# Storing only the two 16x16 diagonal blocks of each Gram product, in place of 32x32 blocks

## The chip, the cores and the metric

The kernel runs on one core of one Trainium2 chip. The metric is the device time of one execution, in microseconds (us). A core has five engines with queues of their own: PE (TensorE, matrix products; PEld is its loading of weights), DVE (VectorE), ACT (ScalarE), POOL (GpSimd) and SP (SyncE, which here only issues transfers). Each works through its instructions in order, and they wait for each other through semaphores. SBUF is the on-chip memory of 128 partitions, PSUM the banks into which PE writes, and DMA engines move data between them and the main memory (HBM).

## The reference

`x` has the shape (16, 64, 256, 256): batch, channels, rows, columns. Two layers are applied:

```
x = x + spectral_conv(group_norm(x))     # FFT, 32x17 modes mixed per head of 16 channels, inverse FFT, bias
x = x + whiten(group_norm(x))            # the last axis (256 columns) in 16 groups of 16
```

The whitening takes, over all batches, channels and rows, the covariance of each group of 16 columns:

```
fg = (x_flat - mean).reshape(16 groups, 16, n)
cov = einsum('gmn,gkn->gmk', fg, fg) / (n - 1)
cov = ((1 - 0.001) * cov + 0.001 * eye) / (n - 1)
out = solve(cholesky(cov), fg)
```

So only 16 blocks of 16x16 are needed of the 256x256 matrix of products of columns (the Gram matrix).

## The kernel before, in words

The kernel has three long stages, with short ones between.

**The first pass** runs over 64 units (a unit is one batch and one head of 16 channels, in 8 pairs). SP loads `x_in` in four parts of 1 MB per unit into one buffer; a part is loaded again as soon as the unit before has used it (`loads`, line 283). For each pair PE makes the Gram products of 32 columns with themselves (`products`, line 421: bank 0 for pairs 0 to 3, bank 1 for pairs 4 to 7), then the transform over rows (line 432) of a sum and a difference of halves that DVE (`halves_sum`, line 854) and POOL (line 768) have made, then the transposes (line 440) and the transform over columns (line 454). Both DVE and POOL may write the halves of pair q only when PE has done line 432 of pair q-2. ACT copies the transformed rows out of PSUM (line 645), DVE the transposes (`xt_copy`, line 860) and, once per unit, the spectrum (`spectrum_kept`, line 866), which PE must have before line 454 of the next unit's first pair. PE runs one pair behind with line 440 and two behind with line 454.

Each unit's Gram products stand in `gram`, 128 partitions x (8 pairs x 2 halves x 32 columns). Partition p holds row p % 32 of a block, and its 32 columns are two runs of 16, of which only one belongs to the row's own group of 16. ACT copies them out of PSUM in two pieces (after pairs 3 and 7) and stores all 512 columns with one transfer at the end of the unit (line 679). Before it overwrites `gram` at pair 3 of the next unit it waits for that transfer and for DVE (`diag_done`). DVE multiplies `gram` by a table of unit matrices (`diagonal`, line 872, at pair 0 of the next unit) and sums the rows (`diagonal_sum`, line 877, at pair 4): the sums of squares for the group norm. At pair 7 ACT issues eight small transfers of the spectrum of the unit before (`spectra_out`, line 653).

DVE's `ch(...)` is an instruction with a wait for its own end behind it, so that the next one may read what it wrote.

**Between**, the modes are mixed, and the second group norm's factors are found.

**The second pass** reads the stored half-transformed rows back (`crs`, SP line 352, two transfers of 512 KB per unit, two buffers), multiplies them on PE (line 525), and reads `gram` back (SP line 356, 256 KB per unit). POOL scales the Gram products by the unit's factors (line 797) and adds them up in `gacc` (line 801). SP's order per unit is: two parts of `crs`, then `gram_in`, for which it waits until POOL is through with the buffer.

**The third pass** loads `x` again, whitens it and stores the output. The change leaves it as it is.

The order on every engine is written out by hand, in the loops shown here.

## Time and profile before

| | |
|---|---|
| median of 3 runs | 3546.78 us (3540.39 to 3562.65) |
| the profiled execution's own time | 3551.07 us |
| its span | 3549.2 us |
| first pass | from the start to about 1141 us |
| second pass | about 1444 to 1706 us |
| third pass | about 1750 us to the end |
| PE, DVE, ACT, POOL busy | 2906.7, 2531.4, 1146.2, 1121.2 us |
| moved by DMA | 1001.81 MB, of it 64 stores and 64 loads of 256 KB for `gram` |

The busy times are sums over the whole span; which engine another waits for is to be read in each pass by itself. A busy time includes the time in which an instruction has been started and is held up.

### The profile page before, as it was taken

What the parts mean: (1) busy time and instruction counts of PE and PEld (TensorE: products, weight loads), DVE (VectorE), ACT (ScalarE), POOL (GpSimd) and SP (SyncE); (2) the same over time, 40 slices, a digit from 0 to 9 for tenths busy, and PEclk for the clock granted to TensorE, in tenths of its full rate; (3) what the DMA queues carried; (4) which work ended last, traced back from release to release, by engine and by line L of the source; (5) the groups of instructions that cost most, each with busy time, mean ns of one, the idle gap of its engine ahead of it and who ended that gap; (6) DMA issues with size and microseconds to landing.
All of it is one profiled execution on the core that took longest, in us unless ns stands there. A gap on an engine that the chain in (4) does not pass through costs nothing.

```text
span 3549.2 us, 230090 instructions
## 1 busy us (share of the span) xinstructions
PE 2906.7 (82%) x98565; PEld 2043.7 (58%) x98565; DVE 2531.4 (71%) x4358; ACT 1146.2 (32%) x2860; POOL 1121.2 (32%) x1434
## 2 busy tenths in 40 slices
PE   4888888888887342466499999999999999999998
PEld 2555555555554331122277777777777777777776
DVE  2777777777777335655477777777777777777777
ACT  0222222222221221000144444444444444444444
POOL 2666666666666112455111111111111111111111
PEclk7999999999999555699799999999999999999999
DMA  9999999999998661699388888888888888888887
GB/s 217 323 330 331 328 331 328 328 331 330 327 328 261 87 91 19 197 339 338 121 302 301 300 303 301 301 301 303 300 301 301 303 301 301 301 303 301 301 302 278
DMA packets 630257, 1001.81 MB, mean 282 GB/s; under 512 B 103712, under 2 KB 464176, under 8 KB 630192
## 3 DMA queue, kind: packets, MB, share of 16 engines
q1 hardware_dynamic: 528816, 912.44, 78.3%
q10 hardware_dynamic: 101376, 88.39, 8.7%
q8 instruction: 55, 0.90, 0.1%
q14 instruction: 10, 0.08, 0.0%
HBM read 639.40 MB, written 361.28 MB: 282 GB/s over the span
## 4 chain that ended last, share of the span: by engine, by line
PE 49%; issue 15%; ACT 14%; ACTq 10%; DMA 6%; DVE 5%; SPq 2%; DVEq 0%; POOL 0%; POOLq 0%
PE bank L593 15%; ACT reg L645 13%; PE bank L584 11%; ACTq L653 6%; PE bank L421 5%; DMA reg<-xh_d 5%; PE bank L432 5%; PE bank L440 3%; PE bank L454 3%; PE bank L564 2%; PE bank L501 2%; PE bank L525 2%; SPq L293 1%; ACT xh L645 1%; PE bank L463 1%
## 5 line engine op out<-in xcount | busy, mean ns | idle before, releaser
L645 ACT ACTIVATE reg<-bank 128x512 f32<-128x512 f32 (+3 forms) x1696 | 844.9, 529 | 1100.9 <-PE bank L593 941.3
L1064 DVE STREAM_TRANSPOSE reg<-bank 128x256 f32<-128x256 f32 x2048 | 737.9, 417 | 336.7 <-PE bank L610 336.7
L768 POOL TENSOR_TENSOR reg<-reg 128x512 f32<-128x512 f32 x512 | 690.0, 1348 | 442.2 <-PE bank L432 386.9
L1068 DVE SCALAR_TENSOR_TENSOR reg<-reg,m,mwhit 128x1024 f32<-128x1024 f32 x512 | 657.6, 1284 | 72.1 <-DVE reg L1064 38.1
L593 PE MATMUL bank<-tab,reg 64*128 64x256 f32 x4096 | 691.9, 404 | 0.0
L822 POOL TENSOR_TENSOR reg<-reg,tab 128x64 f32<-128x64 f32 x512 | 164.2, 321 | 1550.2 <-ACT reg L645 828.5
L854 DVE TENSOR_TENSOR reg<-reg 128x512 f32<-128x512 f32 x512 | 529.1, 1034 | 55.2 <-DMA reg<-in_x_dram 29.7
L610 PE MATMUL bank<-reg 32*32 32x128 f32 x32768 | 547.4, 279 | 1.7 <-DVE reg L1064 1.7
L610 PEld LDWEIGHTS bank<-reg 32*32 32x32 f32 x32768 | 370.8, 103 | 210.3 <-issue 171.5
L584 PE MATMUL bank<-tab,reg 64*128 64x64 f32 x8704 | 443.5, 235 | 46.2 <-ACT reg L645 46.1
L593 PEld LDWEIGHTS bank<-tab,reg 64*128 64x128 f32 x4096 | 458.2, 187 | 27.8 <-issue 0.7
L645 ACT ACTIVATE xh<-bank 128x256 f32<-128x256 f32 x512 | 190.2, 383 | 833.0 <-PE bank L432 730.6
L584 PEld LDWEIGHTS bank<-tab,reg 64*128 64x128 f32 x8704 | 373.0, 147 | 146.5 <-ACT reg L645 112.1
L421 PE MATMUL bank<-reg 128*32 128x32 f32 x32768 | 390.8, 199 | 48.8 <-DMA reg<-in_x_dram 24.6
L860 DVE COPY xht<-bank 128x256 f32<-128x256 f32 x512 | 217.0, 424 | 254.3 <-PE bank L440 248.4
L421 PEld LDWEIGHTS bank<-reg 128*32 128x32 f32 x32768 | 344.2, 110 | 65.4 <-issue 56.3
L432 PE MATMUL bank<-reg,tab 128*32 128x256 f32 x4096 | 332.9, 392 | 6.9 <-issue 5.3
L440 PE MATMUL bank<-tab,xh 128*128 128x128 f32 x1024 | 226.5, 303 | 69.1 <-ACT xh L645 69.1
L440 PEld LDWEIGHTS bank<-tab,xh 128*128 128x128 f32 x1024 | 103.4, 141 | 291.7 <-issue 166.9
L525 PE MATMUL bank<-reg 128*64 128x290 f32 x1024 | 165.9, 454 | 95.1 <-DMA reg<-xh_d 81.2
L572 PE MATMUL bank<-tab,reg 34*128 34x256 f32 x1024 | 228.9, 377 | 0.4 <-ACT reg L645 0.4
L454 PE MATMUL bank<-tab,xht 128*32 128x34 f32 x8192 | 174.1, 202 | 60.3 <-DVE reg L866 54.5
(121 smaller groups left out, 1760.0 us busy)
## 6 DMA issues: line engine op xcount, KB each, us to landing
reg<-in_x_dram SPq DMA_DIRECT2D x256, 1024.0 KB, 8.4
reg<-in_x_dram SPq DMA_DIRECT2D x512, 512.0 KB, 3.9
out_dram<-reg SPq DMA_DIRECT2D x512, 512.0 KB, 2.9
xh_d<-xh ACTq DMA_DIRECT2D x128, 512.0 KB, 7.0
reg<-xh_d SPq DMA_DIRECT2D x128, 512.0 KB, 5.9
gram_d<-gram ACTq DMA_DIRECT2D x64, 256.0 KB
reg<-gram_d SPq DMA_DIRECT2D x64, 256.0 KB, 5.1
spec_d<-psu ACTq DMA_DIRECT2D x512, 8.5 KB
```

What stands on the lines that cost most here:

```text
L421: ins = mm(bank[q // 4][BL * j:BL * j + BL, at:at + BL], blk, blk, start=q % 4 == 0 and half == 0 and c == 0 and t == 0, stop=c == 1 and t ...
L432: ins = mm(bank[2 + q % 2][row:row + KX, 0:W], hc[:, par], halves[:, q % 2, par, c], **one)
L440: ins = mm(bank[4 + q % 2][:, P * half:P * half + P], xh[:, q, P * half:P * half + P], T("eye"), start=half == 0, stop=True, is_transpose= ...
L454: ins = mm(bank[6][BL * j:BL * j + BL, KW * q:KW * q + KW], xht[:, q % 4, half, BL * j:BL * j + BL], wj[:, half], start=q == 0 and half == ...
L584: ins = mm(bank[2 + c][:, at:at + KH], x_re[k, q, r, P * half:P * half + P], T("eye")[k, k], start=half == 0 and r == 0, stop=False, is_tr ...
L593: ins = mm(bank[2 + c][:, H * half:H * half + H], z_sb[k, q // 2, q % 2, P * half:P * half + P], T("hb")[k], start=False, stop=True, skip_ ...
L610: ins = mm(bank[4 + j][BL * i:BL * i + BL, P * half:P * half + P], wp[r, e, half], xt_sb[r, e, half, i // 2].rearrange("p (n h) -> p n h", ...
L645: copy = lambda o, i, **k: nc.scalar.activation(o, i, ACT.Copy, **k)
L768: nc.gpsimd.tensor_tensor(out=halves[:, q % 2, 1], in0=x_in[:, 2 * q:2 * q + 2, 0], in1=x_in[:, 2 * q:2 * q + 2, 1], op=ALU.subtract).then ...
L854: v.tensor_tensor(out=halves[:, q % 2, 0], in0=x_in[:, 2 * q:2 * q + 2, 0], in1=x_in[:, 2 * q:2 * q + 2, 1], op=ALU.add).then_inc(S["sum_m ...
L1064: ins = v.transpose(o_sb[:, q].rearrange("p n (f w) -> p f n w", f=2)[:, :, :, BL * j:BL * j + BL], bank[4 + j][:, 0:W].rearrange("p (f n ...
L1068: v.scalar_tensor_tensor(out=o_sb[:, q], in0=o_sb[:, q], scalar=m1[:, ds(t * 4 + q, 1)], in1=mwhit[:, :].unsqueeze(1).to_broadcast([P, 4, W]),
```

## The change

What is stored shrinks from 2x32 to 2x16 columns per pair: `gram_d`, `gram_in`, `gram_w`, `gacc` and `cov` are half as wide. DVE picks the run of 16 columns that belongs to a row's own group: one instruction multiplies the first run by a column `lo` (1 in partitions of the first 16 of 32, else 0), a second adds the other run times `hi`. Both write `blocks`, one half of `gmask`; the unit matrix is then multiplied into the other half, `diag`. The store moves from the end of the unit to pair 3 of the next one, behind DVE's `blocks_made`; DVE waits for the store of the unit before ahead of overwriting `blocks`. The instruction that adds the last cross terms to `cov` becomes two.

```
-COLS = dict(hc=KH, wj=2 * KW, hb=H, e0=W, e1=W, rot=P, fold=KW + 1, eye=P, eye32=2 * BL, dc=1, hk=1, hh=1,
+COLS = dict(hc=KH, wj=2 * KW, hb=H, e0=W, e1=W, rot=P, fold=KW + 1, eye=P, eye32=2 * BL, eye16=2 * M, lo=1, hi=1, dc=1, hk=1, hh=1,
...
+    put("eye16", np.tile(np.eye(M), (P // M, 2)))
+    low_row = (np.arange(P) % BL < M).astype(float)[:, None]
+    put("lo", low_row)
+    put("hi", 1.0 - low_row)
...
-    gram_d = nc.dram_tensor("gram_d", (NU, P, PAIRS * 2 * BL), f32, kind="Internal").ap()
+    gram_d = nc.dram_tensor("gram_d", (NU, P, PAIRS * 2 * M), f32, kind="Internal").ap()
...
-        gram_in, a = cut(reg3, a, 2, PAIRS * 2 * BL)
-        gram_w, a = cut(reg3, a, PAIRS * 2 * BL)
+        gram_in, a = cut(reg3, a, 2, PAIRS * 2 * M)
+        gram_w, a = cut(reg3, a, PAIRS * 2 * M)
...
-        gacc, a = cut(reg3, a, PAIRS * 2 * BL)
+        gacc, a = cut(reg3, a, PAIRS * 2 * M)
+        diag, blocks = (gmask_f[:, i * 256:i * 256 + 256].rearrange("p (n f b) -> p n f b", f=2, b=M) for i in range(2))
...
+            def gram_out(u):
+
+                act.wait_ge(*nth("blocks_made", u + 1))
+                act.dma_start(gram_d[ds(u, 1)].rearrange("u p a -> (u p) a"),
+                              gmask_f[:, 256:512]).then_inc(S["gram_out"], 16)
...
                     if q % 4 == 3:
                         j = q // 4
-                        if j == 0:
-                            act.wait_ge(*nth("gram_out", u * 16))
-                            act.wait_ge(*nth("diag_done", u))
+                        if j == 0 and not first:
+                            gram_out(u - 1)
...
-                act.wait_ge(*nth("gram_copied", u * 2 + 2))
-                act.dma_start(gram_d[ds(u, 1)].rearrange("u p a -> (u p) a"),
-                              flat(gram[:, :, :])).then_inc(S["gram_out"], 16)
...
+            gram_out(NU - 1)
             spectra_out(NU - 1)
...
                 dve.wait_ge(*nth("gram_copied", u * 2 + 2))
-                ch(v.tensor_tensor(out=gmask[:, :, :], in0=gram[:, :, :],
-                                   in1=T("eye32").unsqueeze(1).to_broadcast([P, PAIRS, 2 * BL]), op=ALU.mult))
-                dve.sem_inc(S["diag_done"], 1)
+                dve.wait_ge(*nth("gram_out", u * 16))
+                g = gram[:, :, :].rearrange("p n (f s b) -> p n f s b", f=2, s=2)
+                ch(v.tensor_scalar(blocks, g[:, :, :, 0], T("lo"), None, ALU.mult))
+                ch(v.scalar_tensor_tensor(out=blocks, in0=g[:, :, :, 1], scalar=T("hi"), in1=blocks,
+                                          op0=ALU.mult, op1=ALU.add))
+                dve.sem_inc(S["blocks_made"], 1)
...
             def diagonal_sum(u):
-                ch(v.tensor_reduce(out=ssq_part[:, ds(u * PAIRS, PAIRS)], in_=gmask[:, :, :], axis=AX.X, op=ALU.add))
+                ch(v.tensor_tensor(out=diag, in0=blocks, in1=T("eye16").rearrange("p (f b) -> p f b", f=2).unsqueeze(
+                    1).to_broadcast([P, PAIRS, 2, M]), op=ALU.mult))
+                ch(v.tensor_reduce(out=ssq_part[:, ds(u * PAIRS, PAIRS)],
+                                   in_=gmask_f[:, 0:256].rearrange("p (n b) -> p n b", b=2 * M), axis=AX.X, op=ALU.add))
...
-            ch(v.tensor_tensor(out=cov[:, :], in0=bank[2][:, 0:2 * BL], in1=covg[:, :], op=ALU.add))
+            cross = bank[2][:, 0:2 * BL].rearrange("p (f s b) -> p f s b", f=2, s=2)
+            c3, g3 = (a[:, :].rearrange("p (f b) -> p f b", f=2) for a in (cov, covg))
+            ch(v.scalar_tensor_tensor(out=c3, in0=cross[:, :, 0], scalar=T("lo"), in1=g3, op0=ALU.mult, op1=ALU.add))
+            ch(v.scalar_tensor_tensor(out=c3, in0=cross[:, :, 1], scalar=T("hi"), in1=c3, op0=ALU.mult, op1=ALU.add))
```

On DVE, in the first pass's loop, from pair 0 of a unit (`gmask<-gram` is `diagonal` of the unit before, the 128x512 from `reg` is `halves_sum` of the next pair, `xht<-bank` is `xt_copy`), before:

```order
L872 TENSOR_TENSOR gmask<-gram,tab 128x512 [waits gram_copied]
L114 REGISTER_ALU
L852 ISA [waits dve_chain]
L853 REGISTER_ALU [waits x_in1]
L854 TENSOR_TENSOR reg<-reg 128x512 [waits xh_mm]
L859 REGISTER_ALU
L860 COPY xht<-bank 128x256 [waits xt_mm]
```

and with the change:

```order
L882 TENSOR_SCALAR gmask<-gram,tab 128x256 [waits gram_out]
L118 ISA
L883 SCALAR_TENSOR_TENSOR gmask<-gram,tab,gmask 128x256 [waits dve_chain]
L118 REGISTER_ALU
L860 ISA [waits dve_chain]
L861 REGISTER_ALU [waits x_in1]
L862 TENSOR_TENSOR reg<-reg 128x512 [waits xh_mm]
L867 REGISTER_ALU
L868 COPY xht<-bank 128x256 [waits xt_mm]
```

One instruction has become two, each of half the length, with one more wait between them, ahead of the halves for pair 2.

On DVE at pair 4 of the unit (`diagonal_sum`), before:

```order
L860 COPY xht<-bank 128x256 [waits xt_mm]
L877 ISA
L877 TENSOR_REDUCE ssq_part<-gmask 128x8
L114 REGISTER_ALU
L854 TENSOR_TENSOR reg<-reg 128x512 [waits xh_mm,x_in3,dve_chain]
```

and with the change:

```order
L868 COPY xht<-bank 128x256 [waits xt_mm]
L888 TENSOR_TENSOR gmask<-gmask,tab 128x256
L118 REGISTER_ALU
L890 ISA [waits dve_chain]
L890 TENSOR_REDUCE ssq_part<-gmask 128x8
L118 REGISTER_ALU
L862 TENSOR_TENSOR reg<-reg 128x512 [waits xh_mm,x_in3,dve_chain]
```

The sum has a product ahead of it now, before the halves for pair 6.

On ACT, at pair 3 of the unit, before:

```order
L669 REGISTER_ALU [waits gram_out]
L670 ISA [waits diag_done]
L645 ACTIVATE gram<-bank 128x256 [waits gram_mm]
L676 ISA [waits xh_copied]
L676 DMA xh_d<-xh 128x1024
```

and with the change:

```order
L664 ISA [waits blocks_made]
L664 DMA gram_d<-gmask 128x256
L680 ISA
L650 ACTIVATE gram<-bank 128x256 [waits gram_mm]
L686 ISA [waits xh_copied]
L686 DMA xh_d<-xh 128x1024
```

The store of the Gram products stands here now, and its wait for an earlier store is gone from ACT.

## Rows read from the trace of the kernel before

**Rows 1.** Windows: us, then busy time of each engine, clock, DMA share, GB/s.
```profile
106.70:1122.70 1016.00, 883.32 (x43343) 569.89 (x43335) 780.52 (x1202) 217.67 (x600) 647.07 (x480) 1.00 1.05 329
1444.00:1706.00 262.00, 166.47 (x1025) 72.27 (x1024) 140.08 (x266) 0.63 (x1) 136.43 (x128) 0.90 0.98 320
```

**Rows 2.** Chain of waits of 580 to 660 us, shares by line.
```profile
by line: PE bank L421 18.6%; ACTq L653 17.5%; PE bank L432 15.4%; PE bank L440 12.1%; issue 11.0%; PE bank L454 8.8%; ACT xh L645 3.0%; DVE reg L866 2.8%; ACTq L679 2.7%; PE bank L463 2.7%; ACTq L676 2.0%; ACT gram L645 0.9%; ACTq L683 0.8%
```

**Rows 3.** Waits of 106.7 to 1122.7 us: sum in us, times, longest.
```profile
ACT gram L645 <- DMA gram_d<-gram: 59.7, 60, 1.8
...
POOL reg L768 <- DMA reg<-in_x_dram: 23.6, 20, 1.5
```

**Rows 4.** Timeline of one unit: start, us, instruction, idle before it.
```profile
614.14 0.68 DVE L872 TENSOR_TENSOR gmask<-gram,tab 128x512 f32<-128x512 f32 x1
...
615.15 0.69 DVE L854 TENSOR_TENSOR reg<-reg 128x512 f32<-128x512 f32 x1 [0.33 <-DVE gmask L872]
615.27 1.70 POOL L768 TENSOR_TENSOR reg<-reg 128x512 f32<-128x512 f32 x1 [1.63 <-PE bank L432]
...
616.53 0.64 PE L432 MATMUL bank<-reg,tab 128*32 128x256 f32 x8
...
617.11 0.44 PE L440 MATMUL bank<-tab,xh 128*128 128x128 f32 x2
...
617.92 0.43 DVE L866 COPY reg<-bank 128x272 f32 x1
...
618.41 0.34 PE L454 MATMUL bank<-tab,xht 128*32 128x34 f32 x16 [0.86 <-DVE reg L866]
```

**Rows 5.** Groups by line, 106.7 to 1122.7 us: busy, mean ns, idle.
```profile
L854 DVE TENSOR_TENSOR reg<-reg 128x512 f32<-128x512 f32 x480 | 497.5, 1037 | 24.4 <-DVE gmask L872 19.0 <-issue 0.3 <-PE bank L432 0.3
```

**Rows 6.** Durations of two instructions over the span, ns min/median/max.
```profile
L999 DVE TENSOR_SCALAR reg<-reg,tab x64: 360/830/1240, 1455.0 to 1698.8; 128x272 f32 x62, 128x272 f32<-128x272 f32 x2
...
L1000 DVE TENSOR_TENSOR reg<-reg,ssq_part x64: 441/442/1180, 1455.7 to 1700.0; 128x272 f32 x62, 128x272 f32<-128x272 f32 x2
```

**Rows 7.** Timeline, DVE and POOL, of an early unit.
```profile
89.00 1.14 DVE L872 TENSOR_TENSOR gmask<-gram,tab 128x512 f32<-128x512 f32 x1
90.46 1.53 DVE L854 TENSOR_TENSOR reg<-reg 128x512 f32<-128x512 f32 x1 [0.33 <-DVE gmask L872]
...
93.48 0.43 DVE L866 COPY reg<-bank 128x272 f32 x1
...
90.16 1.28 POOL L768 TENSOR_TENSOR reg<-reg 128x512 f32<-128x512 f32 x1 [0.58 <-PE bank L432]
```

**Rows 8.** Timeline of the same unit as rows 4, pairs 4 to 6.
```profile
621.59 1.28 POOL L768 TENSOR_TENSOR reg<-reg 128x512 f32<-128x512 f32 x1 [0.41 <-PE bank L432]
...
622.23 0.67 DVE L877 TENSOR_REDUCE ssq_part<-gmask 128x512 f32 x1
...
623.84 1.29 POOL L768 TENSOR_TENSOR reg<-reg 128x512 f32<-128x512 f32 x1 [0.97 <-PE bank L432]
...
624.78 0.64 PE L432 MATMUL bank<-reg,tab 128*32 128x256 f32 x8
```

**Rows 9.** Timeline between the passes: a product with scalar, held up.
```profile
1382.53 4.76 POOL L788 TENSOR_TENSOR reg<-reg 128x2176 f32<-128x2176 f32 x1 [98.01 <-DVEq L981]
1382.56 7.01 DVE L979 SCALAR_TENSOR_TENSOR reg<-reg,tab 128x2176 f32<-128x2176 f32 x1 [0.17 <-DVE reg L979]
```

**Rows 10.** Timeline at the end of the first pass.
```profile
1133.73 12.10 POOL L775 TENSOR_SCALAR reg<-reg,tab 128x2176 f32<-128x2176 f32 x2
...
1139.43 0.75 DVE L872 TENSOR_TENSOR gmask<-gram,tab 128x512 f32<-128x512 f32 x1
```

**Rows 11.** Chain of waits in the second pass, start, us, what.
```profile
1571.77 6.37 DMA reg<-xh_d
...
1579.56 5.97 DMA reg<-xh_d
```

**Rows 12.** DMA issues: KB each.
```profile
gram_d<-gram ACTq DMA_DIRECT2D x64, 256.0 KB
```

More of the change, by code:

```diff
@@ L32 @@
 GROUP = 2 * AREA
-M = 16
 BL = 32
@@ L139, in whiten_kernel @@
     xh_d = nc.dram_tensor("xh_d", (NU, P, PAIRS, W), f32, kind="Internal").ap()
-    gram_d = nc.dram_tensor("gram_d", (NU, P, PAIRS * 2 * BL), f32, kind="Internal").ap()
+    gram_d = nc.dram_tensor("gram_d", (NU, P, PAIRS * 2 * M), f32, kind="Internal").ap()
     spec_d = nc.dram_tensor("spec_d", (2, PAIRS, 2, NU, KX, KY), f32, kind="Internal").ap()
     conv_d = nc.dram_tensor("conv_d", (HEADS, B, 2, 2, KX, PAIRS, KY), f32, kind="Internal").ap()
-    cov_d = nc.dram_tensor("cov_d", (P, 2, BL), f32, kind="Internal").ap()
+    cov_d = nc.dram_tensor("cov_d", (P, 2, M), f32, kind="Internal").ap()
     inv_d = nc.dram_tensor("inv_d", (2 * W // BL, M, M), f32, kind="Internal").ap()
@@ L224, in whiten_kernel @@
         qt, qtp = sb("qt", [KW, KW + 1]), sb("qtp", [KW, P])
-        cov, covg = sb("cov", [P, 2 * BL]), sb("covg", [P, 2 * BL])
+        cov, covg = sb("cov", [P, 2 * M]), sb("covg", [P, 2 * M])
         fac = sb("fac", [M, M])
@@ L365, in _ @@
                     sp.dma_start(aug[g:g + 4, :, 0:M],
-                                 cov_d.rearrange("(q s m) f b -> s f q m b", q=4, s=2)[s, half, :, :, M * s:M * s + M]
+                                 cov_d.rearrange("(q s m) f b -> s f q m b", q=4, s=2)[s, half]
                                  ).then_inc(S["aug_in"], 16)
@@ L905, in _ @@
             with dve.Fori(1, NU - 1) as u:
-                ch.enter(u - 1, 2)
+                ch.enter(u - 1, 4)
                 unit(u)
@@ L1030, in _ @@
             dve.wait_ge(*nth("gram_used", NU))
-            ch(v.tensor_reduce(out=covg[:, :], in_=gacc.rearrange("p (n b) -> p b n", b=2 * BL), axis=AX.X,
+            ch(v.tensor_reduce(out=covg[:, :], in_=gacc.rearrange("p (n b) -> p b n", b=2 * M), axis=AX.X,
                                op=ALU.add))
             dve.wait_ge(*nth("cov_mm", 1))
-            ch(v.tensor_tensor(out=cov[:, :], in0=bank[2][:, 0:2 * BL], in1=covg[:, :], op=ALU.add))
+            cross = bank[2][:, 0:2 * BL].rearrange("p (f s b) -> p f s b", f=2, s=2)
+            c3, g3 = (a[:, :].rearrange("p (f b) -> p f b", f=2) for a in (cov, covg))
+            ch(v.scalar_tensor_tensor(out=c3, in0=cross[:, :, 0], scalar=T("lo"), in1=g3, op0=ALU.mult, op1=ALU.add))
+            ch(v.scalar_tensor_tensor(out=c3, in0=cross[:, :, 1], scalar=T("hi"), in1=c3, op0=ALU.mult, op1=ALU.add))
             ch(v.tensor_scalar(cov[:, :], cov[:, :], (1.0 - EPS_W) / DENOM / DENOM, None, ALU.mult))
-            ch(v.scalar_tensor_tensor(out=cov[:, :], in0=T("eye32"), scalar=EPS_W / DENOM, in1=cov[:, :],
+            ch(v.scalar_tensor_tensor(out=cov[:, :], in0=T("eye16"), scalar=EPS_W / DENOM, in1=cov[:, :],
                                       op0=ALU.mult, op1=ALU.add))
@@ L1041, in _ @@
             ch(v.memset(aug[:, :, M:2 * M], 0.0))
[L1042 to L1043 removed]
+            aug_f = aug[:, :, :].rearrange("p a b -> p (a b)")
+            ch(v.memset(aug_f[:, M:M + (2 * M + 1) * (M - 1) + 1:2 * M + 1], 1.0))
             dve.wait_ge(*nth("aug_in", 16 * 4))
```

13 lines of the change are left out of this document (6 added, 7 removed).

## Prediction

> **What bounds the kernel now.** I read the windows first, since the change touches two passes that need not have the same limit. In [rows 1] the first pass (60 units between the two ends of the window) has PE busy for 883 of 1016 us, DVE for 781, POOL for 647, at the full clock, with DMA at 329 GB/s; the second pass moves 320 GB/s with PE at 166 and DVE and POOL near 140 of 262 us. Both look like a DMA limit. The waits say that only the second is one.
>
> In the first pass nobody but POOL waits for a load of `x` [rows 3], 20 times in 60 units and 23.6 us in all: the loads arrive in time. The chain of waits [rows 2] has PE's products, and 17.5% on ACT's queue at line 653, the eight small transfers at pair 7. So the pass is a loop through engines: ACT issues eight transfers, copies pair 7, PE transposes it, DVE copies the transpose, runs `diagonal`, the halves for pairs 2 and 3, `xt_copy` and the spectrum (L866), and only then PE can do line 454 of the first pair [rows 4] (its last row: 0.86 us idle, released by L866); from there PE runs at its own pace to pair 6, and ACT's transfers start again. One such loop is 1016/60 = 16.93 us. Whatever is put on DVE between the last transpose and L866 lengthens it, unless something there has slack.
>
> In the second pass the chain is nearly all "load of `xh_d`, a few products, load": one loop is two units, 1579.56 - 1571.77 = 7.79 us, of it 6.37 the transfer, 5.97 in the next loop [rows 11]. Two units are four times 512 KB and twice 256 KB [rows 12], 2.62 MB, so 337 GB/s.
>
> **A lock between DVE and POOL.** The argument turns on it. In the early unit of [rows 7] DVE's L854 starts at 90.46, while POOL's L768 runs from 90.16 to 91.44; L854 takes 1.53 us in place of the 0.69 of [rows 4] and ends at 91.99, 0.55 after POOL. So a DVE instruction with two SBUF inputs that comes second is held until POOL's is through. The other way round, POOL's L768 takes 1.70 in place of 1.28 [rows 4, 8] when it comes 0.12 us behind L854. The product with a scalar, L979, is held likewise [rows 9]: 7.01 us, with its end 2.28 us behind POOL's. The one-input product L999 goes from 0.36 to 1.24 [rows 6]. L877, a sum over one input, is not held: 0.67 us though POOL is in its instruction all along [rows 8]. The Trainium skill has this rule in "SBUF — State Buffer", section "Who interferes with whom": the port pair is locked for a whole instruction by whichever comes first, `tensor_scalar` in its two-port mode and anything with two SBUF inputs included, `tensor_reduce` not; by that rule, the trace agrees.
>
> **The parts.**
>
> 1. `diagonal`, at pair 0. Before, with L872's start as 0: it ends at 0.68, the halves for pair 2 start at 1.01 and end at 1.70, and POOL's instruction for pair 3 comes at 1.13, 0.12 too late to be first [rows 4]. Now: the pick by `lo`, 256 columns, at the 0.36 of L999 (272 columns); a wait of the kind between L999 and L1000, taken as 0.13 (0.33 at most, the larger wait in [rows 4]); the second pick with two SBUF inputs, 0.43, from L1000's 0.44; then the same 0.33 as before. The halves for pair 2 start at 1.25. POOL's start hangs on PE's line 432 of pair 1, which hangs on the same transpose and doesn't move: 1.13. POOL is first. It runs unhindered to 1.13 + 1.28 = 2.41, and the halves for pair 2 end at 2.41 + 0.55 = 2.96, where they ended at 1.70. PE's line 432 of pair 2, before at 2.39, now starts at 3.01. The halves for pair 3 need POOL no more and take 0.69 behind a copy, to 4.03; line 440 follows line 432 by 0.58 and L866 follows that by 0.81, as before, and both come out 0.62 late. The early unit, in which POOL was first, shows the same from one end to the other: L866 ends 4.91 behind L872's start, not 4.21, so 0.70. I take 0.65, between the two. [Rows 5] count 480 halves, eight for each of 60 units; with the one that begins as the window ends 61: **+40 us**. The two units ahead of them are in the other order already and get some 0.2 each.
>
> 2. `diagonal_sum`, at pair 4. Counted from L877's start at 622.23 [rows 8]: POOL is in its instruction to 0.64, the new product (two inputs, 256 columns) is held to it and ends 0.28 later, 0.92 (for 512 columns it was 0.55); 0.13 wait; the sum over 256 in place of 512 columns, 0.67 - 0.27 = 0.40; the halves for pair 6 start at 1.48. POOL's next comes at 1.61. DVE is first by 0.13, ends at 2.17, and PE wants these halves at 2.55. So **0**, covered by 0.38 us of PE's own work; if the cover goes, see the second rival.
>
> 3. The store. ACT loses one transfer ahead of the next unit's first copy and gets it at pair 3, where its wait for the earlier store, 59.7 us in 60 units [rows 3], goes. That wait stood beside PE's products, and ACT gram is 0.9% of the chain [rows 2]: nothing. The transfer at the end (L679) is 2.7% of the chain, 2.2 us in the 80 shown, which are 4.7 units: 28 us in 60, if all came back. But what it made late is line 440 of pair 0, and behind that line 432 of pair 2 now waits until 3.01 for DVE's halves, so nothing of it is left. I take **0**, with -10 as the lower end, should PE's earlier start get something past that wait. DVE now waits for the store of the unit before: issued at pair 3, wanted at pair 0 of the next unit, some 10 us later, and the 512 KB loads of [rows 11] land within 6.4. **0.** Behind that wait would stand the halves for pair 2.
>
> 4. The end of the pass. POOL there has two instructions of 6.05 us one behind the other, from 1133.73 to 1145.83 [rows 10]. L872 came at 1139.43, between the two, and got through in 0.75; all DVE work behind it until the next stage had one SBUF input at most. Now the second pick and the product of the sum have two, and come behind the second of POOL's. They are held until 1145.83 and end at 1146.1, where L872 ended at 1140.18: **+6 us**, bounds 0 (if POOL let go between) and +7.
>
> 5. The second pass. Each unit moves 0.131 MB less of 1.31. If bytes set the loop, 0.131 MB at 337 GB/s, times 64, is 24.9 us; if only the 6.17 us of transfer (mean of the two) in a loop shrink by a tenth, 32 x 0.62 = 19.8. I take **-22 us**. POOL's instructions are half as long, and SP, which waits for them ahead of its next load, gets on sooner: no new wait. Were transfers bound by something other than bytes, 0. The Trainium skill, in "DMA: Bandwidth & Descriptors", section "Anatomy of one DMA — SWDGE (gpsimd) path", has a fit of 2.0 us plus bytes/436 GB/s for one transfer of another kind of queue; by it 128 KB less is 0.30 us, 19 us in 64, and the sum would be 3 us higher. No run so far shows which.
>
> 6. One more short instruction on `cov`, under 0.5 us, and the early units: +1.
>
> The sum: 40 + 6 - 22 + 1 = **+25 us**. On the profiled execution's own 3551.07 that is 3576; it lies 4.3 above the median of the runs shown, so on the median 3546.78 it is **3572 us**, +0.7%. (A change under 1%, about 35 us, is not told from none by a measurement of this kernel.)
>
> **The rivals.**
>
> *Second race lost too, slower.* The 0.13 us of part 2 is thin. If the wait in front of the sum is 0.33, or the product takes a little longer, POOL's instruction is first at 1.61, ends at 2.90, and the halves for pair 6 end at 3.45 for a PE that wants them at 2.55: +0.9 us per unit, 61 x 0.9 = 55, which falls into the loop since ACT's transfers start behind pair 6. That gives 3627. It decides from 0.13 us on. For it: the size of the margin; against it: the waits of one kind repeat within hundredths. Chance 0.2.
>
> *First race kept.* If DVE were first at pair 2 after all (picks shorter by 0.12, or POOL later), only 0.24 us of part 1 are left, at most: 61 x 0.2 = 13 in place of 40, 3545. Chance 0.13.
>
> *DMA is the limit of the first pass.* The 329 GB/s of [rows 1] are close to the second pass's 337. Then 0.131 of 16.93 x 0.329 = 5.57 MB per unit goes, 2.4% of 1016 us: -24, and DVE's additions are hidden: 3546.8 - 24 - 22 + 6 = 3507. Against it: [rows 3], the loads are hardly waited for. Chance 0.07.
>
> *No gain in the second pass.* The loop is latency and products, not bytes: 3594. Against it: the rate. Chance 0.08.
>
> *The change doesn't do what it says* can be left out: the order on DVE and ACT shows every step.
>
> **How the numbers follow.** My case has 0.47, and 0.05 are left for what I don't see. Its own range, from part 3, 4 and 5, is 3560 to 3584. The range that holds 8 in 10 must take in the second race, so it is 3540 to 3630; the DMA case lies outside. Faster by over 1% is the DMA case and a little: 0.08. Within 1% (up to 3582) are my case but for its upper end, and the race kept: 0.57. Slower: the race lost, no gain in the second pass, and the upper end: 0.35.
>
> **What would show it.** Part 1: in the first pass's timeline the halves for pair 2 take about 1.7 us behind POOL's instruction of 1.28 us, the unit's loop is 17.6 us, and L866's successor ends 4.85 behind the first pick's start. Part 2: the halves for pair 6 take 0.69 us and POOL's next 1.7. Part 4: a DVE pick of some 6 us at the very end of the pass. Part 5: a second pass of about 240 us in place of 262, at the same GB/s. I am wrong if the loop stays under 17.2 us, or passes 18.2 (the second race), or if the second pass keeps its length.

## The result and the profile after

The changed kernel takes 3619.0 us (median of 4 runs, 3608.5 to 3627.3) where the kernel before takes 3550.4 beside it: a ratio of 1.020, with an interval of 1.018 to 1.022. That is +69 us, or 1.9%, where +25 and a change within 1% were forecast; the stated range, 3540 to 3630, still holds it. The profiled execution took 3627.3 us, its span is 3625.5, 76.3 more than before's 3549.2, and the first pass is now the whole of the difference.

Windows of the changed kernel, the first pass over the same stretch as in [rows 1] and the second pass by its own times (columns as there):

```profile
106.70:1122.70 1016.00, 853.10 (x40570) 549.00 (x40571) 799.98 (x1236) 209.77 (x563) 639.67 (x450) 0.97 1.00 301
1519.00:1790.00 271.00, 180.08 (x1083) 80.33 (x1081) 111.38 (x277) 1.28 (x3) 81.42 (x129) 0.87 0.88 279
```

Two things are to be seen against [rows 1]. The same 1016 us hold 450 of POOL's instructions in place of 480, so a unit takes about 18.1 us, not 16.93; and PE's granted clock is 0.97, not 1.00. The bandwidth has fallen with the pace and with the smaller store, from 329 to 301 GB/s. From the first spectrum copy (L874, before L866) to the last there are 63 units: 18.27 us each, 17.04 before, together +77 us. The last of them holds the end of the pass. The second pass, from PE's first product there to the sum of `gacc`, takes 250.5 us, before 252.6.

**The race at pair 2.** Timeline of the changed kernel, one unit, DVE, POOL and PE (start, us, instruction, idle before it):

```profile
656.50 0.34 DVE L882 TENSOR_SCALAR gmask<-gram,tab 128x256 f32<-128x256 f32 x1
656.87 0.48 DVE L883 SCALAR_TENSOR_TENSOR gmask<-gram,tab,gmask 128x256 f32<-128x256 f32 x1
...
657.63 1.28 POOL L776 TENSOR_TENSOR reg<-reg 128x512 f32<-128x512 f32 x1 [1.41 <-PE bank L437]
657.68 1.78 DVE L862 TENSOR_TENSOR reg<-reg 128x512 f32<-128x512 f32 x1 [0.32 <-PE bank L437]
...
659.56 0.64 PE L437 MATMUL bank<-reg,tab 128*32 128x256 f32 x8 [0.81 <-issue]
...
660.95 0.43 DVE L874 COPY reg<-bank 128x272 f32 x1
...
661.44 0.34 PE L459 MATMUL bank<-tab,xht 128*32 128x34 f32 x16 [0.87 <-DVE reg L874]
```

This answers to [rows 4]. POOL starts 1.13 behind the first pick, DVE's halves 1.18, 0.05 too late: they take 1.78 us in place of 0.69. The spectrum copy ends 4.88 behind the pick's start, where it ended 4.21 behind L872's. The row of L437 has something that [rows 4] do not: 0.81 us of idle time of PE, with 1.0 us of products between it and the 0.87 that was there before as 0.86. Its releaser reads "issue", but it ends at 659.56, 0.1 us behind the end of DVE's held instruction. The order is the rule and not this unit's accident: between 100 and 1080 us DVE comes second at pair 2 in 52 of 54 units of the changed kernel, and in none of 58 before.

**The second race.** The same view at pair 4:

```profile
647.74 0.91 DVE L888 TENSOR_TENSOR gmask<-gmask,tab 128x256 f32<-128x256 f32 x1
648.78 0.42 DVE L890 TENSOR_REDUCE ssq_part<-gmask 128x256 f32 x1
649.24 0.69 DVE L862 TENSOR_TENSOR reg<-reg 128x512 f32<-128x512 f32 x1
649.35 1.73 POOL L776 TENSOR_TENSOR reg<-reg 128x512 f32<-128x512 f32 x1 [0.98 <-PE bank L437]
```

DVE is first, by 0.11 us, and its halves take the free 0.69. It is first in all 54 units between 100 and 1080 us, by 0.09 us or more.

**The clock.** Timeline of PE alone, another unit of the changed kernel:

```profile
605.11 0.64 PE L437 MATMUL bank<-reg,tab 128*32 128x256 f32 x8 [0.80 <-issue]
605.68 0.44 PE L445 MATMUL bank<-tab,xh 128*128 128x128 f32 x2
606.98 0.34 PE L459 MATMUL bank<-tab,xht 128*32 128x34 f32 x16 [0.86 <-DVE reg L874]
...
608.81 0.69 PE L445 MATMUL bank<-tab,xh 128*128 128x128 f32 x2
609.43 0.46 PE L459 MATMUL bank<-tab,xht 128*32 128x34 f32 x16
609.67 1.07 PE L426 MATMUL bank<-reg 128*32 128x32 f32 x64
```

and windows of the same kernel, on either side of that point:

```profile
606.00:607.00 1.00, 0.14 (x5) 0.02 (x3) 0.84 (x3) 0.19 (x1) 1.00 (x1) 1.00 0.91 251
...
608.00:609.00 1.00, 1.00 (x11) 0.19 (x2) 0.00 (x0) 0.07 (x1) 0.02 (x1) 0.50 1.06 339
```

After two idle times of 0.80 and 0.86 us, with 1.0 us of products between them, the granted clock reads 0.50 (1.2 GHz) in place of 1.00 (2.4 GHz), and the same product of L445 takes 0.69, not 0.44. Between 100 and 1080 us the trace has 18 such stretches; the trace of before has none there. Of the 18, 16 begin behind this pair of idle times, and two behind a single one of 1.7 us ahead of L445 of the last pair. So the units come in two kinds: of the 53 whole units of about that stretch, 35 last 17.5 to 18.0 us and 18 last 18.3 to 20.0.

**The end of the pass.** Timeline of DVE and POOL, changed kernel:

```profile
1206.38 11.93 POOL L783 TENSOR_SCALAR reg<-reg,tab 128x2176 f32<-128x2176 f32 x2
...
1211.79 0.88 DVE L882 TENSOR_SCALAR gmask<-gram,tab 128x256 f32<-128x256 f32 x1
1212.71 5.65 DVE L883 SCALAR_TENSOR_TENSOR gmask<-gram,tab,gmask 128x256 f32<-128x256 f32 x1
```

The second pick is held to the end of POOL's pair of instructions, as [rows 10] let expect.

**The store and reload.** DMA issues of the changed kernel (KB each, median us to landing), the first of which answers to [rows 12]:

```profile
gram_d<-gmask ACTq DMA_DIRECT2D x64, 128.0 KB, 2.3
...
reg<-gram_d SPq DMA_DIRECT2D x64, 128.0 KB, 5.8
```

and the waits of SP's queue in the second pass (sum in us, times, longest), before:

```profile
SPq L356 <- POOLq L802: 70.5, 58, 1.9
SPq L352 <- PE bank L525: 62.2, 64, 12.3
```

and with the change:

```profile
SPq L357 <- PE bank L530: 119.9, 99, 11.6
...
SPq L361 <- POOLq L810: 1.1, 6, 0.2
```

SP hardly waits for POOL any more. It waits for PE instead, to be through with the buffers of `crs`, and the sum of its waits has gone only from 133 to 121 us. The loads of `xh_d`, before and with the change (DMA issues, median us to landing):

```profile
reg<-xh_d SPq DMA_DIRECT2D x128, 512.0 KB, 5.9
```

```profile
reg<-xh_d SPq DMA_DIRECT2D x128, 512.0 KB, 6.0
```

There are fewer bytes beside them, and they are no shorter.

### The profile page after: what moved, and what is told of

Read it like the earlier page. It is cut to its first block, busy times and chain, and to the rows that moved or that the text cites. A ratio compares the mean times of both kernels' runs of the same rounds, so it can differ in the third digit from the quotient of the medians.

```text
span 3625.5 us, 230342 instructions
## 1 busy us (share of the span) xinstructions
PE 2949.3 (81%) x98565; PEld 2068.3 (57%) x98565; DVE 2582.5 (71%) x4487; ACT 1152.8 (32%) x2860; POOL 1104.5 (30%) x1434
## 4 chain that ended last, share of the span: by engine, by line
PE 53%; issue 14%; ACT 13%; ACTq 8%; DMA 5%; DVE 5%; SPq 2%; DVEq 0%; POOL 0%; POOLq 0%
PE bank L598 14%; ACT reg L650 12%; PE bank L589 11%; PE bank L426 6%; ACTq L658 6%; PE bank L437 6%; DMA reg<-xh_d 5%; PE bank L445 4%; PE bank L459 3%; PE bank L569 2%; PE bank L530 2%; PE bank L506 2%; SPq L298 1%; PE bank L468 1%; DVE reg L874 1%
## 5 line engine op out<-in xcount | busy, mean ns | idle before, releaser
L776 POOL TENSOR_TENSOR reg<-reg 128x512 f32<-128x512 f32 x512 | 729.3, 1429 | 475.5 <-PE bank L437 438.2
L862 DVE TENSOR_TENSOR reg<-reg 128x512 f32<-128x512 f32 x512 | 579.7, 1132 | 49.8 <-DMA reg<-in_x_dram 26.4
L426 PE MATMUL bank<-reg 128*32 128x32 f32 x32768 | 401.5, 202 | 46.8 <-issue 28.2
L426 PEld LDWEIGHTS bank<-reg 128*32 128x32 f32 x32768 | 354.7, 113 | 63.6 <-issue 54.8
L868 DVE COPY xht<-bank 128x256 f32<-128x256 f32 x512 | 214.4, 419 | 245.4 <-PE bank L445 245.4
L437 PE MATMUL bank<-reg,tab 128*32 128x256 f32 x4096 | 345.7, 404 | 51.3 <-issue 49.6
L445 PE MATMUL bank<-tab,xh 128*128 128x128 f32 x1024 | 232.8, 310 | 64.5 <-ACT xh L650 64.5
L445 PEld LDWEIGHTS bank<-tab,xh 128*128 128x128 f32 x1024 | 106.1, 145 | 293.1 <-issue 178.9
```

Of the source, the lines that this page charges most:

```text
L426: ins = mm(bank[q // 4][BL * j:BL * j + BL, at:at + BL], blk, blk, start=q % 4 == 0 and half == 0 and c == 0 and t == 0, stop=c == 1 and t ...
L437: ins = mm(bank[2 + q % 2][row:row + KX, 0:W], hc[:, par], halves[:, q % 2, par, c], **one)
L445: ins = mm(bank[4 + q % 2][:, P * half:P * half + P], xh[:, q, P * half:P * half + P], T("eye"), start=half == 0, stop=True, is_transpose= ...
L776: nc.gpsimd.tensor_tensor(out=halves[:, q % 2, 1], in0=x_in[:, 2 * q:2 * q + 2, 0], in1=x_in[:, 2 * q:2 * q + 2, 1], op=ALU.subtract).then ...
L862: v.tensor_tensor(out=halves[:, q % 2, 0], in0=x_in[:, 2 * q:2 * q + 2, 0], in1=x_in[:, 2 * q:2 * q + 2, 1], op=ALU.add).then_inc(S["sum_m ...
```

## The experiments

All times in one table. "Unit" is the mean time of the 63 units between the first and the last spectrum copy, "1.2 GHz" the number of stretches at half clock between 100 and 1080 us, "second" the length of the second pass, all three of the profiled execution. The last of the 63 holds the end of the pass, so the 6 us of part 4 are 0.1 us of the change's mean.

| kernel | median us | ratio to before, interval | unit | 1.2 GHz | second |
|---|---|---|---|---|---|
| before | 3549 to 3551 | | 17.04 | 0 | 252.6 |
| the change | 3619.0 | 1.020 [1.018, 1.022] | 18.27 | 18 | 250.5 |
| 1 picks moved | 3546.7 | 0.999 [0.997, 1.001] | 17.04 | 1 | 236.0 |
| 2 half, no picks | 3540.0 | 0.996 [0.994, 0.998] | 17.02 | 0 | 242.8 |
| 3 split only | 3587.6 | 1.010 [1.007, 1.013] | 17.74 | 0 | 245.4 |
| 4 both places filled | 3589.4 | 1.010 [1.006, 1.014] | 17.84 | 0 | 245.4 |
| 5 no reload | 3546.2 | 0.999 [0.998, 1.000] | 17.05 | 1 | 245.2 |
| 6 second pass filled | 3544.2 | 0.998 [0.996, 0.999] | 17.03 | 1 | 244.6 |
| 7 picks moved, spread | 3498.3 | 0.986 [0.983, 0.988] | 16.24 | 0 | 245.1 |
| 8 before, spread | 3552.3 | 1.000 [0.999, 1.002] | 17.13 | 19 | 247.3 |
| 9 before, moved, spread | 3495.6 | 0.984 [0.982, 0.987] | 16.18 | 1 | 247.8 |
| 10 pair 2 filled | 3600.6 | 1.012 [1.008, 1.017] | 17.78 | 0 | 247.9 |
| 11 pair 0 filled | 3619.0 | 1.019 [1.016, 1.022] | 18.17 | 16 | 249.0 |
| 12 = 8, pair 2 filled | 3529.0 | 0.994 [0.992, 0.997] | 16.73 | 0 | 244.2 |

The theory at the outset: the loss is the race at pair 2, plus PE's clock that falls because of the idle time which the lost race makes. Its rival: the rest beyond the race is the work of the picks themselves, or of the moved store.

**1. The picks at another place.** The change, with `diagonal` run at pair 3, between the halves and `xt_copy`.

```
+                    if q == 3 and not first:
+                        diagonal(u - 1)
                     if q >= 1 or not first:
                         xt_copy(...)
-                        if q == 0:
-                            diagonal(u - 1)
-                        elif q == 2:
+                        if q == 2:
                             spectrum_kept(u - 1)
```

> The changed kernel with one move: the two picks stand on DVE at pair 3, between the halves for pair 4 and the copy of the transpose of pair 2, where DVE of the changed kernel idles for 1.1 us per unit. Theory (lost race for the lock at pair 2, and PE's clock falling in the longer idle time behind it): the halves for pair 2 come ahead of POOL again, the loop is at most the 16.9 us of the kernel before, PE's clock stays at full in the first pass, which ends some 70 us sooner than with the change; about 3545 us. Rival (the picks cost by their own length, wherever they stand, or the first pass is slowed by the store's new place on ACT): 3600 to 3620 us.

72 us come back. Timeline of this kernel, DVE and POOL:

```profile
643.45 0.68 DVE L862 TENSOR_TENSOR reg<-reg 128x512 f32<-128x512 f32 x1
...
644.62 1.28 POOL L776 TENSOR_TENSOR reg<-reg 128x512 f32<-128x512 f32 x1 [1.34 <-PE bank L437]
...
648.07 0.34 DVE L882 TENSOR_SCALAR gmask<-gram,tab 128x256 f32<-128x256 f32 x1
...
648.44 0.48 DVE L883 SCALAR_TENSOR_TENSOR gmask<-gram,tab,gmask 128x256 f32<-128x256 f32 x1
```

The halves for pair 2 take 0.68 and are through before POOL comes; the picks, of the same length as in the change, cost nothing here. Place, not work. The store is issued at pair 3 as in the change, so its move costs nothing either.

**2. Half the bytes, nothing else.** Before, with only the first 256 of `gram`'s 512 columns stored, reloaded and summed.

```
-                              flat(gram[:, :, :])).then_inc(...)
+                              flat(gram[:, :, :])[:, 0:PAIRS * BL]).then_inc(...)
```

> The kernel before, with only the first 256 of the 512 columns of the Gram products stored, reloaded and summed (so the covariance leaves out half of them); DVE and ACT as before. Theory: the first pass stays at 16.9 us per unit, since its loads are not what it waits for, and only the second pass moves; if the second pass of the changed kernel is as long as before (250.5 against 252.6 us) because of the shorter transfers and POOL instructions themselves, this is 3545 to 3550 us; if it was PE's clock or something that the change did elsewhere, it gains 20 us: 3525 to 3530. Rival (the DMA engines limit the first pass): 3500 to 3510 us.

The unit stays at 17.02 us: the bytes of the store are not what limits the first pass. The whole gain is 11 us by the medians (3550.6 before), 14 by the ratio, with an interval of 6 to 22: some gain is shown, and probably less than the 22 that the second pass alone was to give.

**3. The race without the picks.** Before, with the product by the unit matrices cut into two.

```
-                ch(v.tensor_tensor(out=gmask[:, :, :], in0=gram[:, :, :], ...))
+                for n in (slice(0, 4), slice(4, 8)):
+                    ch(v.tensor_tensor(out=gmask[:, n, :], in0=gram[:, n, :], ...))
```

> The kernel before, with DVE's product with the unit matrices (128x512) cut into two of 128x256, one behind the other; the same bytes, nothing else. Its halves for pair 2 would start 1.3 us behind the first product's start, not 1.0. Theory (lost race): POOL comes first at 1.13, the halves take 1.7 us, the loop is 17.5 us, PE's clock falls now and then as in the changed kernel, and the time is 3610 to 3625 us. Rival (a little longer DVE work costs its own 0.3 us): 3565 to 3570 us.

Timeline of this kernel:

```profile
655.65 1.28 POOL L768 TENSOR_TENSOR reg<-reg 128x512 f32<-128x512 f32 x1 [1.36 <-PE bank L432]
655.71 1.77 DVE L854 TENSOR_TENSOR reg<-reg 128x512 f32<-128x512 f32 x1 [0.32 <-PE bank L432]
...
655.77 0.44 PE L440 MATMUL bank<-tab,xh 128*128 128x128 f32 x2 [0.22 <-ACT xh L645]
...
657.58 0.64 PE L432 MATMUL bank<-reg,tab 128*32 128x256 f32 x8 [0.52 <-issue]
```

The race is lost by 0.06 us and the kernel is 37 us slower with the same bytes and the same arithmetic: the size of part 1, shown without the change. The clock did not fall, against what I expected; PE's idle time at this place is 0.52 here, not 0.81. In this kernel ACT still has the store to issue at the end of the unit, and L440 waits 0.22 us for it ahead of transposing pair 0; in the change the store is elsewhere, that wait is gone, and PE stands the longer at pair 2.

**4. PE kept busy.** The change, with two needless 128x128 products at each of two places where PE is idle: behind pair 0's products, ahead of transposing the last pair of the unit before, and ahead of the row transform of pair 2.

```
+            def filler():
+                for _ in range(2):
+                    mm(bank[7][:, W:W + P], T("eye"), T("eye"), start=True, stop=True, skip_group_check=True)
...
+                if q == 2:
+                    filler()
                 pe.wait_ge(*nth("xh_copied", u * PAIRS + q - 1))
...
                     products(u, q)
+                    if q == 0 and not first:
+                        filler()
```

> The changed kernel with two needless 128x128 products on PE at each of its two idle places in a unit (behind pair 0's products, ahead of line 437 of pair 2). Theory (of the 1.17 us that a unit takes longer, 0.65 is the race and 0.5 are units in which PE's clock fell to half behind the idle place): the clock stays at full, every loop is 17.5 to 17.6 us, and the time falls by some 30 us to 3585 to 3590. Rival (the clock falls for another reason, or the slow units are slow from something else): 3615 us or more.

More work, 30 us less time. Windows of this kernel in the first pass, beside the changed kernel's:

```profile
100.00:1080.00 980.00, 892.78 (x40532) 590.11 (x40530) 796.49 (x1221) 207.07 (x555) 631.29 (x445) 1.00 1.03 308
```

```profile
100.00:1080.00 980.00, 822.74 (x39082) 529.24 (x39078) 771.25 (x1193) 201.80 (x541) 617.22 (x433) 0.97 1.00 301
```

The filler adds PE work and yet more of POOL's halves are done in the same 980 us, 445 against 433. What differs is the clock column. The race is lost here as before; what is left over experiment 3 (2 us) is within the intervals.

**10 and 11. Which idle time?** Experiment 4 with the filler at one place only: ahead of the row transform of pair 2 (the idle time that the change adds) in 10, behind pair 0's products in 11.

> The changed kernel with two needless 128x128 products per unit at the one idle place of PE that the change has added (ahead of the row transform of pair 2), not at the other (ahead of the column transform of the first pair). Theory: this added idle time is what lets PE's granted clock fall to half; with it filled the clock stays full in the first pass, 3585 to 3595. Rival: the other idle time (0.86 us, there before too) counts as much, and a third or more of the 18 half-clock stretches stay: 3600 to 3620.

> The changed kernel with two needless 128x128 products per unit at the idle place of PE that was there before as well (ahead of the column transform of the first pair), not at the one that the change has added. Theory: the clock falls as in the changed kernel, 3608 to 3622. Rival: the sum of both idle times counts, and filling either one keeps the clock full: 3585 to 3595.

Both expectations take the place of experiment 11's filler for the 0.86 us ahead of the column transform of the first pair. It is not. The edit puts the filler into `if q == 0`, ahead of the transposes of the pair before, and the column transform of the first pair comes two pairs later. Timeline of PE, one unit of experiment 11 (L415 is the filler; its two products are recorded as x4):

```profile
652.48 0.71 PE L415 MATMUL bank<-tab 128*128 128x128 f32 x4
653.43 0.44 PE L449 MATMUL bank<-tab,xh 128*128 128x128 f32 x2 [0.24 <-ACT xh L656]
...
657.31 0.64 PE L441 MATMUL bank<-reg,tab 128*32 128x256 f32 x8 [0.81 <-issue]
...
659.18 0.34 PE L463 MATMUL bank<-tab,xht 128*32 128x34 f32 x16 [0.86 <-DVE reg L880]
```

and of experiment 10:

```profile
712.05 0.71 PE L415 MATMUL bank<-tab 128*128 128x128 f32 x4
712.93 0.64 PE L443 MATMUL bank<-reg,tab 128*32 128x256 f32 x8 [0.17 <-issue]
...
714.80 0.34 PE L465 MATMUL bank<-tab,xht 128*32 128x34 f32 x16 [0.86 <-DVE reg L880]
```

So PE has three idle times in a unit of the change: 0.7 to 1.8 us ahead of transposing the last pair (before it was 0.7 to 1.3), 0.81 at pair 2, 0.86 ahead of the first column transform. Experiment 11 shortens the first of them, and 16 half-clock stretches stay, with the change's own time. Experiment 10 fills the second, leaves the first and the third, and there is no stretch. So the added one tips it, and needless work at another place does not help. The 0.86 us were filled in no experiment: alone they don't bring the clock down (before and experiment 10 have them), but whether the 0.81 would do it without them is not shown. That experiment 11 came out in the range of its theory says nothing of the rival that it was meant to test.

Experiment 10's median is 18 us below the change, not 30; its four runs are 3600.1, 3602.7, 3601.2 and 3575.7, and its interval meets experiment 4's. Its profile has the full clock in the first pass, and a unit of 17.78.

**5. No reload.** Experiment 1, with 8 of the 256 columns of `gram_d` reloaded (and the unit matrix added, so that the rest can be computed).

```
-                    sp.dma_start(gram_in[:, e], gram_d[ds(t * 2 + e, 1)]....
+                    sp.dma_start(gram_in[:, e, 0:8], gram_d[ds(t * 2 + e, 1), :, 0:8]....
```

> The first experiment's kernel (picks at pair 3), but the second pass reloads only 8 of the 256 columns of the Gram products (so the covariance is made of what lies in the buffer, and a unit matrix is added to it to keep it invertible): 64 loads of 4 KB in place of 128 KB, 8 MB less. It asks what bounds the second pass once the loads are halved. Theory (round trips: a load, four products, the next load; bytes count for little): the second pass gets at most 5 us shorter, 3541 to 3547 us. Rival (bytes: the transfers of 128 KB still cost their 0.39 us each): 25 us shorter, some 3522 us.

Windows of the second pass of this kernel, and of the changed one:

```profile
1464.00:1709.00 245.00, 170.26 (x1029) 78.26 (x1029) 101.70 (x256) 0.27 (x1) 80.89 (x127) 0.89 0.86 266
```

```profile
1532.00:1783.00 251.00, 173.38 (x1034) 76.03 (x1034) 99.68 (x258) 0.27 (x1) 80.36 (x127) 0.89 0.92 291
```

Nearly all of the remaining 8 MB are gone and the pass is as long as in experiments 4, 6 and 7; only the bandwidth fell. The time, too, is experiment 1's, 3546.2 against 3546.7. So the bytes of the reload, once they are halved, don't set this pass; those of the loads of `xh_d` were not varied.

**6. PE kept busy in the second pass.** Experiment 1, two needless products ahead of each wait for `xh_d`.

```
                         if q % 4 == 0:
+                            for _ in range(2):
+                                mm(bank[7][:, W:W + P], T("eye"), T("eye"), ...)
                             pe.wait_ge(*nth(f"crs_in...
```

> The first experiment's kernel with two needless 128x128 products on PE ahead of each of the two waits for xh_d in a unit of the second pass, 0.44 us each time by the duration of line 445. It asks what PE's falling clock costs there. Theory (of the 22 us forecast for the second pass about half went to half-clock stretches, 17 to 60 us of them in the profiles so far, at about 0.3 us per us): the clock stays at full in the second pass, which takes some 232 us, and the time is about 3538 us, with less spread. Rival (the clock there costs nothing, the fillers delay the products): the second pass gets longer, 3550 to 3570 us.

The window reads a clock of 0.99 where experiment 1's reads 0.98, and the pass is not shorter (244.6 against 236.0). Experiment 1's profile had the clock nearly full already, so this says little: I can't put a price on the clock in this pass.

**7 and 8. ACT's eight transfers.** The chain of [rows 2] has 17.5% on them, experiment 1's has 21.8%. In 7 they are spread over pair 7 and the first three pairs of the next unit, two at a time, on top of experiment 1; in 8 the same on the kernel before.

```
                     if q == 7 and not first:
-                        spectra_out(u - 1)
+                        spectra_out(u - 1, 0)
...
                     copy(xh[:, q], bank[2 + q % 2][:, 0:W]).then_inc(S["xh_copied"], 1)
+                    if q < 3 and not first and not second:
+                        spectra_out(u - 2, q + 1)
```

> The first experiment's kernel with ACT's eight small transfers of a unit's spectrum spread over four pairs (two at pair 7, two behind the copies of pairs 0, 1 and 2 of the next unit), so that pair 7's copy waits 1 us for them and not 4. Theory (the first pass is a loop through ACT's queue, which stands for 22% of the chain of waits): the loop falls from 17.0 us towards the 16.1 us that 5.44 MB need at 338 GB/s, 50 us less, some 3495 us. Rival (the first pass is at its DMA limit at 323 GB/s already): no more than 10 us less, 3537 or more.

> The kernel before with the same spreading of ACT's eight transfers, Gram products whole as before. With the run beside it, it says what halving the stored products is worth when the loop isn't bound by ACT. Theory: DMA binds here at 5.57 MB per unit, so this is 0.39 us per unit and some 8 us in the second pass slower than the other: 30 us more, some 3525 us. Rival (DVE binds, which has less to do here): the same as the other or faster.

One edit, 48 us in one kernel and nothing in the other. The timeline of experiment 8 tells why:

```profile
654.16 1.28 POOL L776 TENSOR_TENSOR reg<-reg 128x512 f32<-128x512 f32 x1 [1.03 <-PE bank L432]
...
654.81 1.19 DVE L880 TENSOR_TENSOR gmask<-gram,tab 128x512 f32<-128x512 f32 x1
...
655.95 1.28 POOL L776 TENSOR_TENSOR reg<-reg 128x512 f32<-128x512 f32 x1 [0.50 <-PE bank L432]
...
656.32 1.46 DVE L862 TENSOR_TENSOR reg<-reg 128x512 f32<-128x512 f32 x1 [0.33 <-DVE gmask L880]
...
657.88 0.64 PE L432 MATMUL bank<-reg,tab 128*32 128x256 f32 x8 [0.81 <-issue]
```

With PE running sooner, POOL's instruction for pair 2 lies over `diagonal` (L880 takes 1.19, held), the halves for pair 2 lose the race to POOL's next (for pair 3), PE stands idle for 0.81 us, and 19 half-clock stretches follow: units of 16.6 to 16.8 us and units of 17.8 to 17.9. It is the change's own ailment in a kernel that doesn't have the change. The first of the three idle times is missing here (L440 follows at once), so it isn't needed for the fall; and 16 of the 18 distances between the stretches are 51.2 us, which is three units.

**12. The same, with pair 2 filled.** Experiment 8 with experiment 10's filler.

> The kernel before with ACT's eight transfers spread, and two needless 128x128 products per unit in PE's idle time ahead of the row transform of pair 2. Without them this kernel took 3552 us: its units took 16.65 us, or 17.85 where the granted clock fell to half, 19 times in the first pass. Theory: the clock fell because of that idle time, which the spreading brought in by making the race at pair 2 come out for POOL; filled, the clock stays full, and 19 times 1.2 = 23 us go: 3525 to 3535. Rival: the clock stretches come from elsewhere, or the needless products cost as much as they save: 3545 to 3555.

3529.0, inside the theory's 3525 to 3535: 23 us for 19 stretches, 1.2 us each, as the two kinds of unit say.

**9. The full-size store in the best order.** Before, with its one product moved to pair 3 and the transfers spread.

> The kernel before (32 columns per block stored, reloaded and summed, one product with the unit matrices) with that product moved to pair 3, as in the kernel with the moved picks, and with ACT's eight transfers of the spectrum spread. It tells whether the half-size store is worth anything once neither the race nor ACT's transfers hold the loop. Theory: the loads of x then arrive just in time (339 GB/s and 18 waits of POOL for a load in the half-size kernel of the same order, 3498 us), so 0.131 MB more per unit costs part of its 0.39 us in the first pass (+12 to +25 us) and 8 us in the second; 6 us at the end of the pass are saved: 3512 to 3528. Rival: the bytes are hidden in the first pass here too, 3498 to 3506.

3495.6, so the rival had it (and even its 3498 was not low enough): with 64 times 128 KB more each way, it is no slower than experiment 7. Waits of this kernel, 110 to 1080 us, and windows:

```profile
POOL reg L776 <- DMA reg<-in_x_dram: 98.6, 86, 2.9
```

```profile
100.00:1080.00 980.00, 897.67 (x44117) 583.57 (x44117) 845.52 (x1224) 226.13 (x610) 694.53 (x489) 1.00 1.06 347
```

The loads of `x` are waited for now, 98.6 us on POOL against 17.5 in experiment 7, and the bandwidth is up from 338 to 347 GB/s; the extra bytes are carried at a higher rate, not in more time. This kernel and experiment 7 are the fastest of the case, 1.6% and 1.4% under before, and the first of them has nothing of the change in it.

## Why the prediction was right or wrong

Two steps of the sum failed. It has no term for what PE's clock does in the new idle time, which it put at nothing without a reason and which cost some 29 us; and it took 22 us off for the second pass, which became 2 us shorter. The race, which it was built on, came out as forecast.

**Part 1, the race at pair 2: right.** Forecast +0.65 us a unit and +40; the spectrum copy came 0.67 later, and experiment 3, which has nothing but this, cost 37. The pieces also held: the picks 0.34 and 0.48 (forecast 0.36 and 0.43), POOL's start at 1.13, the halves' end at 2.96. DVE's halves came at 1.18 rather than 1.25, so the margin was 0.05, not 0.12. The Trainium skill's rule of "SBUF — State Buffer", section "Who interferes with whom", that whichever comes first locks the port pair for its whole instruction, is borne out: `scalar_tensor_tensor` was held for 5.65 us at the end of the pass, and half a tenth of a microsecond decided 1.1 us of DVE's time.

**Part 2, the second race: right**, won by 0.11 where 0.13 was forecast. The rival in which it is lost said 3627, and the measured 3619 lies closest to it of all the cases. It is wrong all the same: the row at 649.24 shows the race won. A number that fits is no evidence for its mechanism. The same goes for the stated range: it holds the result only because its upper end was stretched to 3630 for this rival, and the prediction's own case ended at 3584.

**Part 3, the store: right as a price**, 0: experiment 1 keeps the moved store and has before's unit, 17.04. But its sentence that nothing is left of PE's earlier start is where a part of the longer idle time comes from, 0.81 in the change against 0.52 in experiment 3. That the moved store is what makes this difference is read from the rows and was not tried alone. **Part 4: right**, +6: L883 ends at 1218.36, where with both picks free it would have ended near 1212.7. Part 6 is too small to be told.

**Part 5, the second pass: mis-sized.** Forecast −22; the profile gave −2. Over all profiles, kernels with the full reload took 252.6, 245.4, 247.3, 247.8 and 244.2 us (mean 247.5), those with half of it 250.5, 236.0, 242.8, 245.4, 244.6, 245.1, 247.9 and 249.0 (mean 245.2), the one with almost none 245.2. So by the profiles the halving takes about 2 us off a length that varies by 10 and more between them, and the rival "no gain in the second pass", given 0.08, is much nearer than the forecast. The times allow more for the halving as a whole: by their ratios experiments 1, 5 and 6 lie 3 to 9 us below before, though each still has the 6 us at the end of the first pass (in experiment 1 the second pick is held for 5.65 us there too), and experiment 2, which hasn't them, lies 14 below. That is 9 to 15 us, each with an interval of some 5 us or more either way; where the rest of it falls is not shown, and between experiments 9 and 7 nothing of it is to be seen.

The step that failed was the sentence that read 337 GB/s as a limit. As the waits read, it is what two buffers of `crs` give when a load of some 6 us has to be used before the next may be sent; this reading was not tested by itself. The estimate by the Trainium skill's fit in "DMA: Bandwidth & Descriptors", section "Anatomy of one DMA — SWDGE (gpsimd) path", 0.30 us a unit or 19 us in all, is above both figures. For the reload, 5.8 us to landing at 128 KB, experiment 5 shows that the path gains nothing when it is nearly gone.

**What the sum left out: PE's clock in the first pass.** The prediction lists PE's later start at pair 2 (3.01 in place of 2.39) and says in the next breath only what it does to the loop. It never asks what PE does in between: it is idle, for 0.81 us, close ahead of an idle time of 0.86, and the granted clock then fell 18 times. +77 us for 63 units, less 6 for the end and about 42 for the race (63 x 0.67), leaves 29; experiment 4 took 30 back. That is the larger part of the miss: 40 + 29 + 6 − 2 = 73 (64 with 11 for the halving), against 69 measured by medians and 76 by the spans. [Rows 1] had the clock at 1.00, so no fall of this kind was to be seen before; but the 0.90 of the second pass, in the same rows, showed that this kernel's waits can bring it down.

**Rivals.** The first race kept, and DMA as the limit of the first pass, are out (the timeline above; experiment 2's unit of 17.02). Of the signs of being wrong, the second pass that keeps its length was met. The loop that passes 18.2 was so only by the mean of 18.27 with the end of the pass in it; by the window that gave 16.93 before it is 18.06, where 17.6 was forecast, and the reason is not the second race that the sign names.

**Open.** Why the clock falls in 18 of the units and not in the others of the change, why in experiment 8 it does so in every third, and why an idle time of 0.52 (experiment 3) does not bring it down at all: the runs show which idle time matters, not a rule. That the second pass is set by waits for buffers is supported only from one side (fewer bytes of the reload don't help); a third buffer of `crs` was not tried.

## What to carry to other kernels

Where one engine's instruction holds up another's, as DVE's and POOL's do here, an instruction split in two or put a little later can lose a race that an unchanged duration says nothing of: compare starts, not only durations, and move the work to where the other engine is far off. Price a new idle time of PE twice, once for itself and once for the clock that follows. A bandwidth near its best seen value is no proof of a limit: ask whether the next transfer was waiting to be sent, or not yet allowed to be. And look in the trace whether a filler stands in the idle time that it was meant for.

## What the runs showed of the hardware that was not expected

- PE's granted clock went to 0.50 after idle times of 0.81 and 0.86 us with 1.0 us of products between them, 16 times in the change and 19 times in experiment 8, and never in the first pass of experiment 3, where they were 0.52 and 0.86. Each such stretch cost 1.2 us in experiment 8. Two needless products, 0.71 us per unit, in the first of these idle times made the kernel 18 us (experiment 10) and 23 us (experiment 12) faster.
- A `tensor_scalar` of 256 columns that met POOL's long instruction took 0.88 in place of 0.34 us (it got through between the two of POOL's pair), and the `scalar_tensor_tensor` behind it 5.65 us in place of 0.48.
- The first pass ran at 347 GB/s in experiment 9; the prediction had read 337 as a limit in the second pass.
